# Four groups of row scatters instead of sixteen in a row, in the third expert layer of a twelve-stage kernel

## The reference

```python
T = xt.shape[0]                                  # 1024
capacity = int(T / E * CAP_F)                    # 160
gate_logits = xt @ Wg + bg
top_v, top_i = jax.lax.top_k(gate_logits, TOPK)  # TOPK = 2
expert_label = jax.nn.one_hot(top_i, E, dtype=xt.dtype).sum(axis=1)
seq = jnp.cumsum(expert_label, axis=0) * expert_label
valid = (seq > 0) & (seq <= capacity)
slot = (seq - 1.0).astype(jnp.int32)
flat_idx = jnp.where(valid, arange(E)[None, :] * capacity + slot, E * capacity)
src = jnp.broadcast_to(xt[:, None, :], (T, E, d)).reshape(-1, d)
buf = jnp.zeros((E * capacity + 1, d)).at[flat_idx.reshape(-1)].set(src)
disp = buf[:-1].reshape(E, capacity, d)
h = silu(einsum('ecd,edh->ech', disp, W1)) * einsum('ecd,edh->ech', disp, W2)   # h: 1024 wide
out = einsum('ech,ehd->ecd', h, W3)
...
y = (softmax(top_v)[:, :, None] * sel).sum(axis=1)   # sel: the two experts' rows of each token
```

## Time and profile before

| | us |
|---|---|
| median of 3 runs (2733.12 to 2735.02) | 2733.4 |
| the profiled execution, its own time | 2737.03 |
| its span in the trace | 2735.2 |
| PE busy | 2549.4 (93%) |
| POOL busy | 625.9 (23%) |
| stage `L2_ffn` from the first scatter to the last addition | 1705.3 to about 1856 |

### The profile page before, as it was taken

The page is one execution under the profiler, slowest core; times in us unless marked ns, Lnnn a source line. Parts: engine busy times, 40 slices in busy tenths (PEclk is TensorE's granted clock), DMA queues, the critical chain, the costliest instruction groups (busy, mean ns, idle before and its releaser), DMA issues. The chain is left out here.

```text
span 2735.2 us, 47273 instructions
## 1 busy us (share of the span) xinstructions
PE 2549.4 (93%) x18498; PEld 1961.7 (72%) x18498; DVE 1457.3 (53%) x2400; ACT 994.4 (36%) x2147; POOL 625.9 (23%) x649
## 2 busy tenths in 40 slices
PE   8889996999999898979999997888999999989999
PEld 4566993666666656957888886885888886367778
DVE  4484224777777733035555457225555554379982
ACT  2252224666666421332222221123222222377741
POOL 2002002010101001013333330112333332047833
PEclk9999998999999998989999998999999999999999
DMA  9443873111110103942121112553112211012210
GB/s 294 128 138 117 301 265 94 47 33 32 47 32 17 51 1 132 330 140 74 59 70 62 55 36 107 187 195 110 60 59 68 70 58 41 1 62 85 85 43 16
DMA packets 97803, 260.04 MB, mean 95 GB/s; under 512 B 19028, under 2 KB 45368, under 8 KB 90184
## 3 DMA queue, kind: packets, MB, share of 16 engines
q1 hardware_dynamic: 86520, 240.17, 26.4%
q0 software_dynamic: 3840, 10.49, 1.2%
q10 hardware_dynamic: 7248, 6.65, 0.7%
HBM read 236.13 MB, written 21.14 MB: 94 GB/s over the span
## 5 line engine op out<-in xcount | busy, mean ns | idle before, releaser
L2191 POOL TENSOR_TENSOR buf<-buf 128x512 f32<-128x512 f32 x128 | 159.9, 1273 | 504.9 <-ACT buf L2325 504.9
L2350 DVE TENSOR_REDUCE buf<-acc 128x256 f32<-128x1024 f32 x128 | 150.7, 1219 | 219.0 <-PE acc L2218 219.0
L2251 PE MATMUL acc<-buf 128*128 128x256 f32 x1024 | 257.2, 384 | 3.6 <-ACT buf L2334 3.6
L2212 PE MATMUL acc<-buf 128*128 128x256 f32 x1024 | 236.6, 384 | 3.5 <-PEq L89 2.6
L2319 ACT COPY buf<-acc 128x256 f32<-128x256 f32 x64 | 23.8, 372 | 533.5 <-PE acc L2233 533.5
L2212 PEld LDWEIGHTS acc<-buf 128*128 128x128 f32 x1024 | 189.4, 190 | 36.9 <-issue 12.1
L2251 PEld LDWEIGHTS acc<-buf 128*128 128x128 f32 x1024 | 180.8, 190 | 37.5 <-issue 15.9
L2719 ACT ACTIVATE buf<-acc,buf 128x512 f32<-128x512 f32 x256 | 172.4, 685 | 75.1 <-DVE buf L2753 75.1
L2753 DVE TENSOR_REDUCE buf<-acc 128x1 f32<-128x512 f32 x256 | 158.9, 682 | 63.5 <-PE acc L2631 63.5
L2363 DVE TENSOR_TENSOR buf<-acc,buf 128x1024 f32<-128x1024 f32 x128 | 150.7, 1219 | 67.8 <-ACT buf L2319 67.8
L2643 PEld LDWEIGHTS acc<-identity,buf 128*128 128x128 f32 x1024 | 114.3, 141 | 84.0 <-issue 78.2
(11 more groups left out here) (420 smaller groups left out, 4802.4 us busy)
## 6 DMA issues: line engine op xcount, KB each, us to landing
buf<-in_L_ffn_W SPq DMA_DIRECT2D x52, 1024.0 KB, 6.8
buf<-in_ctx SPq DMA_DIRECT2D x48, 768.0 KB, 4.3
buf<-in_ctxT SPq DMA_DIRECT2D x64, 512.0 KB, 3.8
buf<-in_L_ffn_w SPq DMA_DIRECT2D x36, 704.0 KB
buf<-state_rows SPq DMA_DIRECT2D x32, 512.0 KB
buf<-in_ctxT SPq DMA_DIRECT2D x96, 128.0 KB, 4.1
buf<-in_L_ffn_w SPq DMA_DIRECT2D x18, 640.0 KB
buf<-in_ctxT SPq DMA_DIRECT2D x32, 256.0 KB, 5.3
```

The costliest lines, as they stand in the source:

```text
L2191: pool.tensor_tensor(quarters[:, 2 * n:2 * n + 2, :], t[:, 4 * n:4 * n + 2, :], t[:, 4 * n + 2:4 * n + 4, :], ALU.add).then_inc(adding, 1)
L2212: pe.matmul(acc_s[:, n, :], ct0[x][:, tile(key_tile(n))], q0[:, b, 4 * y:4 * y + 4, :], start=(n % 2 == 0), stop=False)
L2251: pe.matmul(acc_m[:, 0:ROWS], ctx[x][:, key_tile(n), 0:P], probsT[y][:, n, :], start=(n == 0), stop=(n == KT - 1))
L2350: dve.tensor_reduce(most_of[n][:, :], acc_s[:, 4 * n:4 * n + 4, :].rearrange("p k r -> p r k"), AX.X, ALU.max).then_inc(part_most, 1)
```

## The change

After every second tile, that is after scatters 4, 8, 12 and 16, POOL now waits until all scatters issued so far have landed. Nothing else differs.

```diff
@@ -1662,6 +1662,8 @@
                     for k in range(K):
                         pool.indirect_dma_start(chip.slots_sent, bass.IndirectOffsetOnAxis(to_int[:, k, j:j + 1], axis=0),
                                                 xn[:, j, :], None).then_inc(scattered, 16)
+                    if j % 2:
+                        pool.wait_ge(scattered, 16 * K * (j + 1))
                 pool.wait_ge(found, 1)
```

## The result

| | before | with the change |
|---|---|---|
| median of 6 runs each, us | 2734.18 | 2721.85 |
| lowest and highest | 2730.87, 2738.15 | 2719.94, 2730.44 |
| span of the profiled execution | 2735.2 | 2728.6 |
| first scatter to first down product of expert 0 | 30.95 | 20.80 |
| first scatter to last addition of the stage, start to start | 150.2 | 139.8 |

The ratio is 0.9961 with a 95% interval of 0.9948 to 0.9973: 10.7 us faster, between 7.4 and 14.2. The spans differ by only 6.6, because this execution came to its first scatter 5.0 us later, in stages that the change doesn't touch. So the stage is read from its own first scatter. From there to the first down product it is 1736.25 - 1705.30 before and 1731.11 - 1710.31 now.

The account below looks back on a forecast made before the run. PE was taken as the bound, idling in expert 0 because its news arrives late beside POOL's scatters. Some 5.3 us of gaps and 3.1 of clock gave -8.4 from the median 2733.4: 2725.0 us, own range 2722 to 2728, 8 in 10 2721.5 to 2737.5.

Parts of the forecast that it names:

- What bounds the stage: Third expert layer: PE is the bound; its 8.3 us of idle time in expert 0's up products lie on the path.
- PE's news of a finished piece is held while POOL issues scatters: Expert 0's up products: PE's raising of `up_filled` arrives late, about one in 5.0 us, during sixteen scatters.
- News held in group 2 drains at 1716.7 + 2.7 = 1719.4: Scatters 5 to 8: pieces two to five are held, then told 2.7 us after the group's end, although group 3 has begun.
- three bounds: Held news in a group: no hold at all, drained 2.7 us after each group, or no draining before the end, 1731.9.
- the first rival: Groups of four never build up a hold; down products start 11.0 us earlier, 2722.4 us; chance 0.12.
- Sum: Expert 0's down products start at 1727.8 instead of 1736.25, and the gain stays to the end: -8.4 us.
- The clock term: PE at half clock from 1722.25 to 1732.50 after idle time; full clock gives 3.1 us of the 8.4.
- The branch of -6.7: A remaining PE gap of 2.6 us still brings half clock: 3.4 us of it cost 1.7, so -6.7 us.
- Length of the pauses: POOL between groups: 1.48 us instead of 0.30, as SP waits for the last scatter; stream 3.5 us longer, costing nothing.
- Second rival: The hold keeps one news in 5.0 us (+0.7, 2734.1), or is much smaller unprofiled (within 1 us); chance 0.22.
- Third rival: The pace of 5.0 us stays and each pause lets one more news through: -2.7, about 2729 us; chance 0.15.
- fourth, slower: One news per group of four scatters, which the pause stretches to 6.25 us: +3.6, 2737.0, up to 2740; chance 0.18.

Follow-up runs that it names:

- four scatters only: Kernel before with scatters 5 to 16 left out, so its result is not the reference's; 2724.28 us, before 2740.71.
- one pause: Kernel before with POOL waiting for the landing only after scatter 4, then twelve scatters in a row; 2737.28 us, before 2739.09.
- Two groups of eight: Kernel before with POOL waiting for the landing after scatters 8 and 16; single run 2721.71 us, before 2740.71; timed later on another chip, ratio 0.9999.
- pairs: Kernel before with POOL waiting for the landing after every two scatters; 2731.50 us, before 2739.09.
- the repeat: The change itself without edits, timed again beside kernel before; 2723.28 us against 2737.71, ratio 0.9949.
- two kernels that pause in this layer alone: Kernel before with landing waits after scatters 8 and 16, or with a fill of 1024 columns between groups of four; 2724.8 and 2725.9 us, before 2725.7.
- at most four under way: Kernel before with each scatter waiting until the one four before it has landed, on four semaphores; 2730.13 us, before 2740.71.
- the first seven experiments: Seven kernels with one run each, with fewer scatters, other pauses or a limit on scatters under way, beside kernel before; 2721.71 to 2738.71 us.

## Why the prediction was right, point by point

- **What bounds the stage.** Right. PE's gaps in expert 0 were on the path: 10.15 us less to the first down product gave 10.4 us less for the stage, and 10.7 in the timed runs.
- **PE's news of a finished piece is held while POOL issues scatters.** Right, and shown: with four scatters only, and with any pause of 1.13 us or more after every four, it is gone; at 0.39 us it is back. "What PE waits for is not work but news of work" was all of it in kernel before; with one pause only PE also stood still by itself.
- **"News held in group 2 drains at 1716.7 + 2.7 = 1719.4".** This step failed. Nothing was held in a group of four, so nothing had to drain. I took the middle of three bounds from the 2.7 us that a full drain took after the last scatter. The lower bound, "no hold at all in a group", is what happened: the first rival, to which I gave 0.12, and its 2722.4 is the measured 2721.85. Its evidence was the better: news in the fifth scatter at 1711.28 in time, and beside the gathers. Two groups of eight show the drain itself: 1.21 us after the last scatter, in a pause of 1.73, so 2.7 was no minimum either. The prediction's own had said so: there the held news came 1.54 us after the last scatter's end, and "both rows of a full drain have the same 2.7" left that row out.
- **Sum.** -8.4 against -10.7 measured: the missing part is the gap of 2.6 us that the failed step left in PE. That makes 11.0, the first rival's sum; the traces have 11.29 from the first up product on, and 10.15 after the 1.1 us of slower clock before it. The clock term was right: 1.0 in the window in which it was 0.5. The branch of -6.7 did not come about, and no row shows its 3.4 us of half clock; the rows have 10.25 us at 0.50 before and none behind the first up product now.
- **The number.** 2721.85 lies just outside the forecast's own range (2722 to 2728) and 0.35 us inside the range for 8 in 10. It lies inside because that range was drawn down to the first rival. To that extent it was luck; the path, the cause and the sign were not.
- **Length of the pauses.** 1.48 each was the term; measured 1.72, 3.18 and 1.73. POOL saw a landing 0.24 us later than SP did; why one took 3.18 stays open. `tokens(2)` went out 27.46 us after the first scatter instead of the predicted 25.4 (before 21.78). It cost nothing, as put, but of the "over 10 us" from the issue to PE's want 6.8 were left, and 4.5 after the landing; pairs used them up and paid 3.50.
- **Second rival, "pace unchanged, or not there in timed runs"** (0.22). In both timed comparisons of the change it is wrong: the time fell by as much as the trace says (10.7 us), and by 14.0 in the repeat. Its second half is not refuted, since the profiler recorded the timed runs too. On one chip the rival is right for another reason than I gave: no trace shows a hold there, and two kernels that pause in this layer alone gained nothing (0.9999 and 0.9992). The change itself was not run on that chip.
- **Third rival, in between** (0.15), **and fourth, slower** (0.18). Wrong for the change: no news kept a pace in groups of four. The fourth's premise, one news in four scatters, was never put to the test: the stretched groups held nothing. In other kernels with the scatters' cadence unchanged the steps were 2.8 to 5.7 us, so neither a fixed 5.0 us nor four scatters is a law.
- **The rule of the Trainium skill** ("TensorE: Matmul & The Clock Gate", section "The cost: per-tile semaphore tail"): a piece has one increment and not eight (`up_filled` is raised at its last product), so by the rule's 26 ns the estimate is 0.03 us and not the prediction's 0.2. Where there is no hold the trace agrees, PE's news being in ACT 0.03 us after PE's end. The hold of 4.7 us is outside it.

What stays open is what holds PE's increments: which part of POOL's work (writing the addresses of rows, or the DMA engines that read them) is in the way, whether the profiler's own recording has a part in it, why one gets through in some 5 us, why PE itself stood still in one trace, and why one chip of the four with a known number is free of it. Nothing here tells these apart. The scatters' own transfers do not differ: twelve of them are 1.70 MB and 26.4% of the DMA engines' time before, and 26.5% on the chip without the hold. No kernel tried a pause after five or six scatters, nor one between 0.39 and 1.13 us.

## What to carry to other kernels

When an engine waits for something that the profile shows as finished long ago ("remote", or a producer whose records ended microseconds before), look at what else is going on at that time, not at the producer: here it was a third engine's stream of indirect DMAs. Breaking such a stream into runs of four with about a microsecond between them cost nothing that could be measured as long as its last landing had cover, and in the traces a fill does it as well as a wait; where the rows are wanted soon, as in the first two layers, the wait itself cost time (measured on a chip without the hold only). Compare a gain of this kind on more than one chip, and read in an untouched part of the same trace whether the effect is there at all. Here all times come from runs that the profiler recorded.

## What the runs showed of the hardware

- Semaphore increments of PE's products arrived late, by the trace's own record of the raises, while POOL issued indirect DMAs every 1.26 us: by 4.7 us for the second piece of kernel before, by 11.9 us for the fourth (made at about 1716.4, silu at 1728.32), by 6.1 us in the second layer. In a long run they came some 5 us apart (13.75 and 18.74 us after the first scatter before, 13.56 and 18.50 with at most four under way), with single steps from 2.8 to 5.7 us. ACT's and DVE's own increments in the same stretch were acted on in 0.03 to 0.1 us.
- It starts in the fifth to eighth DMA of a run and is cleared by 1.13 us without one, not by 0.39 us.
- In one trace (one pause, after scatter 4) PE's own products stood still under it: seven records in the 6.3 us up to 1733.33, at a granted clock of 0.96, until the held news was told.
- In the second layer it was in ten traces (before, the change twice, the first seven experiments). It was in neither of the two traces of another chip with the same code in that layer, and kernel before was 8 to 15 us faster there than elsewhere.
- Where the hold was, part of the records of semaphore raises by the scatters was missing (62 of 256 kept before, 131 with the change); on the chip without it all 256 were there in each of four traces.
- A scatter of 128 rows of 1 KB had landed for POOL 1.72 to 1.75 us after its instruction's end in most pauses, 2.3 to 3.2 us after it in some; beside a load of weights POOL waited 5.59 us for four.
